# Routed attention: where the softmax division is applied, and how the out-projection is split

## What is computed

```python
dist = jax.nn.softmax(jnp.mean(x @ Wr + br, axis=1), axis=-1)
_, idx = jax.lax.top_k(dist, N_ACTIVE)          # 4 of 16
...
Qs, Ks, Vs = (gather(Q), gather(K), gather(V))  # (2, 4, 512, 64)
score = jax.nn.softmax(jnp.einsum('bhqd,bhkd->bhqk', Qs, Ks) * scale, axis=-1)
O = jnp.einsum('bhqk,bhkd->bhqd', score, Vs)
O = O.transpose(0, 2, 1, 3).reshape(b, s, N_ACTIVE * D_ATTN)
return O @ Wo + bo
```

## Time and profile before

| | us |
|---|---|
| median of 3 runs | 563.67 (563.59 to 565.5) |
| profiled execution, whole | 562.91 |
| its span in the trace | 560.9 |
| PE busy in the span | 480.3 (86%) |
| DVE busy | 384.7 (69%) |
| ACT busy | 269.0 (48%) |
| POOL busy | 155.1 (28%) |
| the routed attention's units, first scores to last addition | 182.9 to 243.9 |

### The profile page before, as it was taken

How to read it: one execution, slowest core, us unless ns; L and a number is a source line. 1 busy time by engine, 2 the same in 40 slices (tenths; PEclk the granted TensorE clock), 3 DMA queues, 4 the chain that set the end, 5 groups by cost and what they waited for, 6 DMA issues and landing times. The chain is left out here.

```text
span 560.9 us, 9297 instructions
## 1 busy us (share of the span) xinstructions
PE 480.3 (86%) x3121; PEld 336.1 (60%) x3121; DVE 384.7 (69%) x1365; ACT 269.0 (48%) x819; POOL 155.1 (28%) x185
## 2 busy tenths in 40 slices
PE   2940699999979999988886958989999999889987
PEld 2410599897634666775555436756666666658945
DVE  3799979844683767844779476863543646789876
ACT  2798488512325666613455334642222221679643
POOL 4999983031135400002104440111000000020042
PEclk9755579999999999997898889999999999989999
DMA  7104000002191000000012300000000000000001
GB/s 264 58 1 150 1 4 1 2 0 71 81 384 46 2 1 2 1 2 1 0 35 58 90 1 1 2 0 2 2 0 1 0 1 1 1 1 1 2 0 39
DMA packets 8453, 18.37 MB, mean 33 GB/s; under 512 B 1171, under 2 KB 6611, under 8 KB 7894
## 3 DMA queue, kind: packets, MB, share of 16 engines
q1 hardware_dynamic: 8406, 17.78, 9.0%
HBM read 15.99 MB, written 1.79 MB: 32 GB/s over the span
## 5 line engine op out<-in xcount | busy, mean ns | idle before, releaser
L212 POOL TENSOR_SCALAR rtmp<-mv 128x4 f32<-128x4 f32 x18 | 4.4, 246 | 240.2 <-DVE mv L191 209.6
L1875 PEld LDWEIGHTS bank<-arenaA,arenaB 128*128 128x128 f32 x320 | 38.7, 192 | 8.4 <-issue 7.2
L1859 PE MATMUL bank<-xnT,arenaA 128*128 128x512 f32 x80 | 41.1, 595 | 0.7 <-ACT xnT L270 0.7
L1886 ACT ACTIVATE xt<-bank 128x512 f32<-128x512 f32 x26 | 15.6, 599 | 54.3 <-PE bank L1859 53.1
L1937 DVE TENSOR_TENSOR arenaB<-xt,bank 128x512 f32<-128x512 f32 x26 | 17.8, 686 | 34.5 <-PE bank L1860 31.8
L1860 PE MATMUL bank<-xnT,arenaA 128*128 128x512 f32 x80 | 40.9, 592 | 0.0
L1875 PE MATMUL bank<-arenaA,arenaB 128*128 128x128 f32 x320 | 38.8, 275 | 0.0
L263 PE MATMUL bank<-in_ctx 128*128 128x512 f32 (+1 forms) x94 | 32.3, 485 | 0.0
L1100 DVE TENSOR_REDUCE nmax<-bank 128x1 f32<-128x512 f32 x32 | 20.5, 684 | 13.2 <-PE bank L1043 13.2
L428 DVE MATCH_REPLACE8 arenaB<-arenaB 128x77 f32<-128x77 f32 x128 | 26.8, 222 | 0.0
L1860 PEld LDWEIGHTS bank<-xnT,arenaA 128*128 128x128 f32 x80 | 15.2, 190 | 19.1 <-issue 19.1
(11 more groups left out here) (486 smaller groups left out, 1306.9 us busy)
## 6 DMA issues: line engine op xcount, KB each, us to landing
arenaA<-in_moe_dram SPq DMA_DIRECT2D x1, 3840.0 KB, 11.6
in_dft<-in_dft_dram SPq DMA_DIRECT2D x1, 2048.0 KB, 7.5
in_dft<-in_head_dram SPq DMA_DIRECT2D x1, 2048.0 KB, 7.6
arenaA<-in_l_dram SPq DMA_DIRECT2D x1, 2048.0 KB, 16.1
vw_scratch<-in_dft SPq DMA_DIRECT2D x32, 38.5 KB
arenaB<-vw_scratch SPq DMA_DIRECT2D x2, 576.0 KB, 4.9
in_rows<-in_rows_dram SPq DMA_DIRECT2D x1, 842.5 KB, 7.3
in_ctx<-in_ctx_dram SPq DMA_DIRECT2D x1, 653.0 KB, 6.3
```

The costliest lines, as they stand in the source:

```text
L1859: nc.tensor.matmul(bank[n % 2][:], w[:, c * P:(c + 1) * P], xnT[:, b * S:(b + 1) * S], start=True, stop=True).then_inc(up_mm, 1)
L1875: ins = nc.tensor.matmul(bank[4 + m % 2][:, q4 * P:(q4 + 1) * P], hid2[:, m % 2, c, q4 * P:(q4 + 1) * P], w[:, 2 * HE + c * P:2 * HE + (c ...
L1886: nc.scalar.activation(sil2[n % 3], bank[n % 2][:], ACT.Silu).then_inc(silu_ready, 1)
```

## The change

The output of PV is no longer divided by the sum of its exponentials on the way. ACT copies it raw from PSUM to `oT0` (the copy of the spread reciprocal is gone, and this one stands behind the exponentials, not ahead of them). The out-projection is done head by head: four matmuls over 64 rows each, into banks 7 (even heads) and 3 (odd heads). VectorE then multiplies each head's projection by that head's 1/sum per token and adds it, four `scalar_tensor_tensor` instructions in a chain, each linked to the one before, and this block stands behind the copy of bank 4. The spreading matmuls, their copy and the product on DVE are gone. Bank 3 is taken from the scores, which now go round banks 0, 1 and 2; PV's output has bank 6 alone. Counts of `rb_copy` and `rb_mm` in a later stage that used the same semaphores are lowered to match.

```diff
@@ -1027,6 +1026,8 @@
                 ins.then_inc(v_ready, 1)
 
         NU = NT * 2
+        score0 = lambda n, i: bank[(2 * n + i) % 3]
+        Y0 = lambda i, c: bank[3 + 4 * (1 - i)][:, c * P:(c + 1) * P]
         AT_O, AT_R, AT_W = slice(0, P), slice(P, 2 * P), slice(2 * P, 3 * P)
 
         def pe_attend0(pe):
@@ -1036,47 +1037,38 @@
                 if n < NU:
                     t, pair = n // 2, n % 2
                     b = t // TB
-                    if n >= 2:
-                        pe.wait_ge(sc_exp, 2 * (n - 1))
                     for i in range(2):
+                        if 2 * n + i >= 3:
+                            pe.wait_ge(sc_exp, 2 * n + i - 2)
                         r = slice(DF * i, DF * (i + 1))
-                        nc.tensor.matmul(bank[2 * (n % 2) + i][:], qT[r, b, pair, (t % TB) * P:(t % TB + 1) * P],
+                        nc.tensor.matmul(score0(n, i)[:], qT[r, b, pair, (t % TB) * P:(t % TB + 1) * P],
                                          kT[r, b, pair, :], start=True, stop=True).then_inc(sc_mm, 1)
                 if n == 1:
                     pe_v0(pe, 1)
                 m = n - 2
                 if 0 <= m < NU:
                     t, pair = m // 2, m % 2
-                    own, other = bank[6 + m % 2], bank[6 + (m + 1) % 2]
-                    pe.wait_ge(rinv_ready, m + 1)
-                    if m:
-                        pe.wait_ge(o_norm, m)
-                    else:
-                        pe.wait_ge(v_ready, 4)
-                    for i in range(2):
-                        h = 2 * pair + i
-                        ins = nc.tensor.matmul(other[DF * i:DF * (i + 1), AT_R], rinv0[:, t, h:h + 1].broadcast_to([P, DF]), ident,
-                                               start=True, stop=True)
-                    ins.then_inc(rb_mm, 1)
                     pe.wait_ge(pT_dve, m + 1)
                     pe.wait_ge(pT_act, m + 1)
                     if m:
-                        pe.wait_ge(rb_copy, m)
-                    if pair and t:
-                        pe.wait_ge(x_added, t)
+                        pe.wait_ge(oT0_copy, m)
+                    else:
+                        pe.wait_ge(v_ready, 4)
                     for k in range(TB):
                         for i in range(2):
                             h = 2 * pair + i
-                            ins = nc.tensor.matmul(own[DF * i:DF * (i + 1), AT_O], vv0[:, t // TB * TB + k, h * DF:(h + 1) * DF],
+                            ins = nc.tensor.matmul(bank[6][DF * i:DF * (i + 1), 0:P], vv0[:, t // TB * TB + k, h * DF:(h + 1) * DF],
                                                    pT0[:, m % 2, i, k * P:(k + 1) * P], start=(k == 0), stop=(k == TB - 1))
                     ins.then_inc(pv_mm, 1)
                 if 2 <= m <= NU and m % 2 == 0:
                     t = m // 2 - 1
-                    pe.wait_ge(o_norm, m)
-                    pe.wait_ge(rb_copy, min(m + 1, NU))
+                    pe.wait_ge(oT0_copy, m)
+                    if t:
+                        pe.wait_ge(x_added, t)
                     for c in range(2):
-                        ins = nc.tensor.matmul(bank[7][:, AT_W], oT0[:, (2 * t + c) % 4, :], wo0[:, c * P:(c + 1) * P],
-                                               start=(c == 0), stop=(c == 1))
+                        for i in range(2):
+                            r = slice(DF * i, DF * (i + 1))
+                            ins = nc.tensor.matmul(Y0(i, c), oT0[r, (2 * t + c) % 4, :], wo0[r, c * P:(c + 1) * P], start=True, stop=True)
                     ins.then_inc(wo_mm, 1)
                 m = n - 1
                 if 0 <= m < NU:
@@ -1097,7 +1089,7 @@
                     for i in range(2):
                         h = 2 * pair + i
                         dve.wait_ge(sc_mm, 2 * n + i + 1)
-                        Vv.tensor_reduce(nmax0[:, t, h:h + 1], bank[2 * (n % 2) + i][:], AX.X, ALU.max, negate=True).then_inc(sc_max, 1)
+                        Vv.tensor_reduce(nmax0[:, t, h:h + 1], score0(n, i)[:], AX.X, ALU.max, negate=True).then_inc(sc_max, 1)
                 m = n - 1
                 if 0 <= m < NU:
                     t, hs = m // 2, slice(2 * (m % 2), 2 * (m % 2) + 2)
@@ -1105,25 +1097,25 @@
                     Vv.reciprocal(rinv0[:, t, hs], rsum0[:, t, hs]).then_inc(rinv_ready, 1)
                 if n == 1:
                     vec_v0(dve, 1)
-                m = n - 2
-                if 0 <= m < NU:
-                    dve.wait_ge(rb_copy, m + 1)
-                    dve.wait_ge(pv_mm, m + 1)
-                    if m >= 4:
-                        dve.wait_ge(wo_mm, m // 2 - 1)
-                    Vv.tensor_tensor(oT0[:, m % 4, :], bank[6 + m % 2][:, AT_O], rb0[:, m % 2, :], ALU.mult).then_inc(o_norm, 1)
-                if 2 <= m <= NU and m % 2 == 0:
-                    t = m // 2 - 1
-                    if t == 0:
-                        dve.wait_ge(row_added, 2)
-                    dve.wait_ge(wo_mm, t + 1)
-                    Vv.tensor_tensor(X[:, t, :], bank[7][:, AT_W], tmp[:, t, :], ALU.add).then_inc(x_added, 1)
                 m = n - 1
                 if 0 <= m < NU:
                     dve.wait_ge(sc_turned, 2 * m + 1)
                     if m >= 2:
                         dve.wait_ge(pv_mm, m - 1)
                     Vv.tensor_copy(pT0[:, m % 2, 0, :], bank[4][:]).then_inc(pT_dve, 1)
+                m = n - 2
+                if 2 <= m <= NU and m % 2 == 0:
+                    t = m // 2 - 1
+                    if t == 0:
+                        dve.wait_ge(row_added, 2)
+                    dve.wait_ge(rinv_ready, 2 * t + 2)
+                    dve.wait_ge(wo_mm, t + 1)
+                    for h in range(4):
+                        ins = Vv.scalar_tensor_tensor(X[:, t, :], Y0(h % 2, h // 2), rinv0[:, t, h:h + 1],
+                                                      X[:, t, :] if h else tmp[:, t, :], ALU.mult, ALU.add)
+                        if h < 3:
+                            st.link(ins)
+                    ins.then_inc(x_added, 1)
 
                 if n == 2 * TB + 3:
                     dve.wait_ge(x_added, TB)
@@ -1137,12 +1129,6 @@
 
         def act_attend0(act):
             for n in range(NU + 2):
-                m = n - 2
-                if 0 <= m < NU:
-                    act.wait_ge(rb_mm, m + 1)
-                    if m >= 2:
-                        act.wait_ge(o_norm, m - 1)
-                    nc.scalar.copy(rb0[:, m % 2, :], bank[6 + (m + 1) % 2][:, AT_R]).then_inc(rb_copy, 1)
                 if n < NU:
                     t, pair = n // 2, n % 2
                     if n >= 2:
@@ -1150,8 +1136,14 @@
                     for i in range(2):
                         h = 2 * pair + i
                         act.wait_ge(sc_max, 2 * n + i + 1)
-                        nc.scalar.activation(pb0[:, n % 2, i, :], bank[2 * (n % 2) + i][:], ACT.Exp, bias=nmax0[:, t, h:h + 1],
+                        nc.scalar.activation(pb0[:, n % 2, i, :], score0(n, i)[:], ACT.Exp, bias=nmax0[:, t, h:h + 1],
                                              accum_out=rsum0[:, t, h:h + 1]).then_inc(sc_exp, 1)
+                m = n - 2
+                if 0 <= m < NU:
+                    act.wait_ge(pv_mm, m + 1)
+                    if m >= 4:
+                        act.wait_ge(wo_mm, m // 2 - 1)
+                    nc.scalar.copy(oT0[:, m % 4, :], bank[6][:, 0:P]).then_inc(oT0_copy, 1)
                 m = n - 1
                 if 0 <= m < NU:
                     act.wait_ge(sc_turned, 2 * m + 2)
@@ -1695,7 +1687,7 @@
                     pe.wait_ge(p2_dve, t + 1)
                     pe.wait_ge(pc2_act, t + 1)
                     if t:
-                        pe.wait_ge(rb_copy, NU + t)
+                        pe.wait_ge(rb_copy, t)
                     for k in range(TB + 1):
                         for h in range(H2):
                             if k < TB:
...
```

9 lines of the change are left out of this document (4 added, 5 removed).

## The result

| | before | after |
|---|---|---|
| median of 4 runs each, us | 564.59 (563.59 to 565.5) | 570.4 (569.93 to 572.4) |
| span of the profiled execution | 560.9 | 568.4 |
| first scores to last addition | 60.96 | 66.27 |
| behind it, to the span's end | 317.01 | 319.37 |

The ratio is 1.0123, with a 95% interval from 1.0092 to 1.0154: about 6.9 us slower, between 5.2 and 8.7. The forecast was 567.7 us with a range up to 570.0. So the direction was right, and the time lies above the range. Of the 7.5 us by which the two spans differ, 5.31 lie in the routed attention and 2.36 behind it; the first scores come 0.17 us earlier.

The account below looks back on a forecast made before the run. PE was taken to set the routed attention's pace, with DVE and ACT close behind. The terms 1.7 - 0.8 + 0.3 + 1.0 + 0.6 + 1.2 gave +4.0 on 563.7, so 567.7 us, range 564.9 to 570.0.

Parts of the forecast that it names:

- Start, +1.7: Stage start: fourth score matmul waits for the first exponential to free bank 0, so V starts 1.7 us later, uncovered.
- Turns 2 to 4, -0.8: Early turns of the stage: three spreading pairs at 0.27 us fall away with no addition block yet, -0.8 us.
- Five tiles, +0.3: Five tiles between the PVs at 195.64 and 231.37: 7.20 us each against 35.73 in all before, +0.3 us.
- The chain: Steps from one even turn's PV through block, maxima, exponentials and ACT's copies to the next, summed to 7.20 us per tile.
- rival 3: Out-projection's four matmuls do not overlap and take 1.10 us, not 0.55: 571.6 us in all, chance 0.08.
- Turn 12, +1.0: Turn 12: normalisation of four tiles, 1.02 us, stands ahead of the maxima and is no longer covered, +1.0 us.
- Last tile but one, +0.6: PV at 231.37 to PV at 237.98: 6.61 us before, the chain still takes 7.20, +0.6 us.
- End, +1.2: Stage end: the last addition, 0.29 us, becomes four linked ones of 1.48 us with nothing to hide them, +1.2 us.
- PE's gain: Per tile in the stage: without two spreading pairs at 0.27 us, PE alone would need 6.61 us instead of 7.15.
- Signs: Expected in the changed profile, among others: PE idle about 0.6 us before each even turn's PV from turn 6 on.
- rival 1: Links between the additions are free: block 1.06 us, tile 6.84, 565.1 us in all, chance 0.22.
- rival 2: PE stays the bound: tile 6.61 us, 563.0 us in all, no change to slightly faster, chance 0.08.

Follow-up runs that it names:

- e2: The changed kernel with the stage's fourth score matmul in bank 3, so that it waits for no exponential: ratio to before 1.0085, stage 64.42 us.
- e6: The changed kernel with projection and additions per head pair, fourth score matmul in bank 3, next layer's moments and normalisation by single tiles: ratio to before 1.0018.
- e7: The changed kernel with additions in halves, fourth score matmul in bank 3, single-tile moments and normalisation, last tile's first pair projected early: ratio to before 1.0013.
- e3: The changed kernel with the four additions unlinked, three heads' products put in scratch and left out of the result: ratio to before 1.0047, tile 6.97 us.

## Why the prediction was right or wrong

The way the slowdown comes about was foretold, its size was not. Two steps failed. The sum kept TensorE's groups at their old times, the out-projection at 0.55 us above all; it measured 0.64, and the PE groups together make 1.2 of the 1.3 us by which the stage came out longer than forecast. And the sum and the range had nothing for what lies behind the stage, where the other 1.6 us of the 6.9 are. In order:

**Start, +1.7: right.** Measured +1.85, and e2 takes back the same 1.85.

**Turns 2 to 4, -0.8: right.** Measured -0.71 (from V's start to the first PV with a projection, 10.79 to 10.08).

**Five tiles, +0.3: the term that was mis-sized.** Without the extra of turn 12 it measured 5 x 7.36 - 35.73 = +1.07. The mechanism was as foretold: DVE late at the odd turn's maxima, ACT's copy of bank 5 last before the even PV, the step of a link 0.38, the block 1.41 for 1.42. The chain is 7.36 where I summed 7.20. The sizes that missed are on PE: the out-projection 0.64 instead of 0.55, PV 1.03 instead of 0.97, and transposes to copy 0.70 instead of 0.64. The first is the step "I take 0.55, since the four in rows 8 alternate between halves just as these do". The row of 0.53 had 77 stationary columns, and the doubt stood in the text under rival 3, but only as all or nothing. It came out at a sixth of the way, for which there was no term. The second could be read in the kernel before, from the PV at 237.98, which PE starts after 0.35 us of idle time and not directly behind the spreading pair. PE timeline before, what stands around it, and a group of transposes behind an odd turn's PV:

```profile
237.19 0.44 PE L1058 MATMUL bank<-in_ctx,rinv 128*64 128x128 f32 x4
...
239.00 0.71 PE L1078 MATMUL bank<-in_small,arenaB 128*128 128x128 f32 x4
```

```profile
214.72 1.09 PE L1089 MATMUL bank<-in_ctx,arenaB 128*128 128x128 f32 x8
215.75 1.13 PE L1043 MATMUL bank<-arenaB 64*128 64x512 f32 x4
```

That PV takes 1.02 us to its out-projection (237.98 to 239.00), not 0.97. The transposes show the same: 1.03 us behind an odd turn's PV (214.72 to 215.75), and 0.97 behind the out-projection (211.45 to 212.42). In these rows a group is about 0.05 us shorter when it stands directly behind one of the same array tile (`128*64` behind `128*64`, `128*128` behind `128*128`). The changed kernel fits that: scores over 64 rows now stand ahead of every PV, the out-projection over 64 rows ahead of the transposes, and both take 1.02 to 1.03; only the first transposes, behind V over the whole array, still take 0.97 (188.36 to 189.33). No run tested that this is the reason.

**Turn 12, +1.0: right.** Measured 8.37 - 7.36 = +1.01, with the normalisation 1.03 us long ahead of the maxima; with the moments and the normalisation in single tiles it is gone (e6, e7).

**Last tile but one, +0.6:** measured +0.75, the same 0.16 of the tile. **End, +1.2:** measured +1.36. The block itself was 247.53 to 249.03, 1.50 us for 1.48. The rest lies in front of it: the two out-projections of this end take 0.10 and 0.08 longer to what follows, the transposes to the last PV 0.05, and ACT's raw copy, put at nothing, gives back 0.08 against DVE's product.

Together the stage grew by 1.85 - 0.71 + 1.07 + 1.01 + 0.75 + 1.36 = 5.3 us, where the sum was 4.0. The other 1.6 us of the 6.9 lies behind the stage (2.36 in the first pair of profiles, 1.3 in the means of all). There the prediction had no term at all and gave no reason for that, and its range had none for it either. With the measured stage alone the time would have been about 569, inside the range; that stretch took it out.

**PE's gain was overrated.** PE alone was to need 6.61 per tile and needs 6.86. Of the 0.54 us of spreading matmuls removed per tile, 0.10 went to the out-projection, 2 x 0.05 to the PVs and 0.05 to the transposes behind the out-projection. That leaves 0.29, which is why even e7, with hardly any wait left, gains only 0.86 us on the stage.

**Signs.** PE's idle time in front of the even PVs shows as 0.24 us, not 0.6, and by my own sign ("less than 0.3: rival 1") would have pointed to the wrong case. The second score matmul, which waits for an exponential, stretches its group and hides half of it. I had said that this wait is covered, which holds for the time, but not for what the trace shows. Rival 1 falls by e3, rival 2 by the tile of 7.36, rival 3 by the out-projection of 0.64.

## What to carry to other kernels

- Moving work from the bounding engine to one with idle time helps only if it does not land in front of what the bounding engine waits for: the same four additions cost 7.36 us per tile ahead of the maxima and 6.90 split in two. Follow the chain through the new place before counting the saving.
- When a small instruction group is removed, look up how the groups next to it run in a place where they already lack that neighbour. And a range for the whole kernel must hold what its untouched part does from one execution to the next.

## What the runs showed of the hardware

- A link between neighbouring `scalar_tensor_tensor` of 128x128 costs 0.12 us: a step of 0.38 linked and 0.26 unlinked.
- Four matmuls over 64 rows with 128 stationary columns, 128 columns each, take 0.64 us where two over 128 rows took 0.55; a pair of them alone takes 0.42. In these rows half the rows on alternating halves is thus not quite free, and the short group costs more per matmul than the long one.
- Eight transposes took 0.97 us directly behind a group of the same array tile and 1.03 behind one of another; for a PV of eight matmuls it was 0.97 and 1.02. It is a regularity of these rows; the reason was not tested.
- One stretch of equal work varies by 1.7 us between executions, 19.27 at a granted clock of 1.00 and 20.96 at 0.92, in either kernel.
- The output transfers at the end took 7.75 or 7.76 us in seven executions and 8.5 to 8.8 in five, with equal computing beside them.
